# A causal attention with per-query maxima: scores in fp32r head pairs, double-bank exponentials and one loading queue

## The reference

```
q, k = rope(split_heads(x @ Wq.T + bq)), rope(split_heads(x @ Wk.T + bk))   # 16 heads of 16
v    = split_heads(x @ Wv.T + bv)
att  = softmax(causal_mask(q @ k.T / 4))
y    = (att @ v) @ Wo.T + bo
x    = layernorm(x + y)
h    = silu((x @ w1.T) * s1) * ((x @ w2.T) * s2)           # 1024 wide
h    = gelu((h @ h1.T) * hs1); h = gelu((h @ h2.T) * hs2)
out  = layernorm(x + (h @ w3.T) * s3)
```

## Time and profile before

| | |
|---|---|
| median of three runs | 3186.88 us (3184.31 to 3187.11) |
| profiled execution, first to last instruction | 3187.4 us (it has no other time of its own) |
| mean granted TensorE clock | 0.951 of full speed |
| projection | 0 to about 172 us |
| stacks loaded, TensorE idle | to 238 us |
| row scores alone | 238 to 329 us |
| groups of the attention | 329 to 1966 us |
| feed-forward stages | to 3187 us |

### The profile page before, as it was taken

How to read it: one execution, slowest core, us unless ns; L and a number is a source line. 1 busy time by engine, 2 the same in 40 slices (tenths; PEclk the granted TensorE clock), 3 DMA queues, 4 the chain that set the end, 5 groups by cost and what they waited for, 6 DMA issues and landing times. The chain is left out here.

```text
span 3187.4 us, 51027 instructions
## 1 busy us (share of the span) xinstructions
PE 2923.3 (92%) x15876; PEld 1538.9 (48%) x15876; DVE 2145.0 (67%) x3822; ACT 1310.6 (41%) x2546; POOL 145.8 (5%) x215
## 2 busy tenths in 40 slices
PE   8909999999999999999999997399999995799998
PEld 4402333333333333333333332277777774688887
DVE  7919888888888878888788885655555551434433
ACT  0000677777777766777767764011111110011010
POOL 0070000002000020000200000000000000000000
PEclk9955999999999999999999998699999998899999
DMA  5488000007100062000340001211111003121200
GB/s 158 151 112 99 9 8 5 5 5 81 32 5 5 6 68 45 5 5 6 47 63 8 5 6 64 92 53 53 53 53 53 33 34 127 59 74 39 79 14 20
DMA packets 80648, 146.59 MB, mean 46 GB/s; under 512 B 27452, under 2 KB 50876, under 8 KB 76840
## 3 DMA queue, kind: packets, MB, share of 16 engines
q0 software_dynamic: 11440, 45.43, 10.5%
q1 hardware_dynamic: 60344, 77.47, 7.2%
q10 hardware_dynamic: 8640, 20.85, 2.0%
HBM read 92.67 MB, written 51.04 MB: 45 GB/s over the span
## 5 line engine op out<-in xcount | busy, mean ns | idle before, releaser
L477 DVE TENSOR_REDUCE at_segmax<-at_row 128x1 f32<-128x512 f32 (+3 forms) x2464 | 1414.3, 636 | 315.5 <-PE at_row L393 181.3
L550 ACT ACTIVATE at_probs<-at_key 128x512 f32<-128x512 f32 (+3 forms) x2304 | 1141.9, 566 | 626.6 <-PE at_key L411 349.8
L393 PE MATMUL at_row<-at_k_stack,at_q_stack 96*128 96x512 bf16 (+3 forms) x2464 | 910.4, 378 | 98.5 <-DMA at_k_stack<-k_parts 75.2
L411 PE MATMUL at_key<-at_q_stack,at_k_stack 99*128 99x512 bf16 (+3 forms) x2304 | 831.4, 363 | 4.1 <-issue 1.6
L393 PEld LDWEIGHTS at_row<-at_k_stack,at_q_stack 96*128 96x128 bf16 x2464 | 237.2, 98 | 785.7 <-DVE at_segmax L477 590.9
L428 PE MATMUL at_o<-at_probs,at_values 128*32 128x512 f32 (+3 forms) x4608 | 572.7, 569 | 1.4 <-issue 0.7
L411 PEld LDWEIGHTS at_key<-at_q_stack,at_k_stack 99*128 99x128 bf16 x2304 | 225.8, 98 | 145.9 <-ACT at_probs L550 16.8
L1005 PE MATMUL na_h<-na_h_h,na_h2w_h 128*128 128x512 f32 x512 | 203.3, 397 | 46.2 <-DVE na_h_l L1058 46.2
L1043 ACT ACTIVATE na_h3f<-na_h,na_hs 128x512 f32<-128x512 f32 x64 | 44.0, 688 | 442.6 <-PE na_h L1005 442.6
L739 PE MATMUL wi_f<-wi_h_h,wi_h1w_h 128*128 128x512 f32 x512 | 207.4, 405 | 10.5 <-DVE wi_h_l L870 10.5
L1005 PE MATMUL na_h<-na_h_l,na_h2w_h 128*128 128x512 f32 x512 | 203.2, 397 | 0.0
(11 more groups left out here) (109 smaller groups left out, 2578.6 us busy)
## 6 DMA issues: line engine op xcount, KB each, us to landing
hidden<-wi_h SPq DMA_DIRECT2D x64, 256.0 KB, 2.0
na_h2f<-hidden SPq DMA_DIRECT2D x8, 2048.0 KB, 8.4
at_q_stack<-q_parts POOLq DMA_DIRECT2D x120, 128.0 KB, 25.5
at_k_stack<-k_parts POOLq DMA_DIRECT2D x30, 512.0 KB, 30.6
outputs<-at_outs POOLq DMA_DIRECT2D x32, 256.0 KB, 2.3
wi_o<-outputs SPq DMA_DIRECT2D x8, 1024.0 KB, 5.8
q_parts<-pr_parts SPq DMA_DIRECT2D x48, 128.0 KB, 1.9
k_parts<-pr_parts SPq DMA_DIRECT2D x48, 128.0 KB, 2.2
```

The source lines that it names most:

```text
L393: last = nc.tensor.matmul(bank[:, 0:w], qst[u][0:SROWS, c, h, i * P:(i + 1) * P], kst[u][0:SROWS, h, s * CH:s * CH + w], start=True, stop= ...
L411: last = nc.tensor.matmul(bank[:, q0:CH], kst[u][0:SROWS + PARTS, h, j * P:(j + 1) * P], qst[u][0:SROWS + PARTS, c, h, q0:CH], start=True, ...
L477: nc.vector.tensor_reduce(segmax[:, r, s:s + 1], row_ps[slot][:, 0:w], op=ALU.max, axis=AX.X).then_inc(rows_taken, 1)
L550: nc.scalar.activation(probs[:, g % RING_P, h, q0:CH], key_ps[(QUAD * g + h) % RING_S][:, q0:CH], ACT.Exp).then_inc(probs_ready, 1)
```

## The change

`project` splits q and k into two fp32r parts (high and low) instead of three bf16 ones, and stores them with 4 bytes an element. GpSimd also makes a tile of ones that is stored to DRAM.

`attend` is rewritten:

- `TERMS` are three (high by high, high by low, low by high): 48 rows for a head. Two heads lie over each other, at partitions 0 and 64, so a quad is two pairs. The stacks are fp32r. The maxima are two more rows (high, low) at 48 and 112.
- A key unit is a pair of heads: two matmuls into the two banks of one double bank, then one exponential over both (1024 columns). There are two double banks. Row units stay single, the two heads of a pair alternating, with three banks. Masks are bf16 as before.
- `values` follows two groups behind the keys instead of one, with four buffers of exponentials.
- The maxima are split on GpSimd, turned by VectorE (`transpose` of 32 x 32 blocks, six row units after the last one of the chunk), and stored by SyncE with four DMAs and loaded with two.
- All loads of stacks, ones and values move from GpSimd's queue to SyncE's. The first quad comes in pieces of 512 tokens, then quad 1 whole; only then follow the stores of maxima in SyncE's list.
- The quads run alternately up and down over the chunks. The order of row units and key pairs is worked out by a function `interleave` with fixed costs per instruction: at a chunk's first group all row units still missing for that chunk are issued, and further ones as long as a bank is free while the keys wait.
- There are no hardware loops in the attention: all is written out.

```diff
-PARTS = 3
-TERMS = [(0, 0), (0, 1), (1, 0), (1, 1), (0, 2), (2, 0)]
+PARTS = 2
+TERMS = [(0, 0), (0, 1), (1, 0)]
+RING_R = 3
+RING_K = 2
+PAIRS_G = QUAD // 2
+RING_P = 4
+VALUE_LAG = 2
...
+        parts = sb("parts", [P, 2, PARTS, CH], F32R)
...
-                            nc.vector.tensor_tensor(rest[:, :], full[:, :], parts[:, s, 0, :],
-                                                    ALU.subtract).then_inc(step, 1)
-                            dve.wait_ge(step, steps + 3)
-                            nc.vector.tensor_copy(parts[:, s, 1, :], rest[:, :]).then_inc(parts_ready, 1)
-                            dve.wait_ge(parts_ready, it * 4 * PAIRS + 2 * m + 1)
-                            nc.vector.tensor_tensor(parts[:, s, 2, :], rest[:, :], parts[:, s, 1, :],
+                            nc.vector.tensor_tensor(parts[:, s, 1, :], full[:, :], parts[:, s, 0, :].bitcast(F32),
                                                     ALU.subtract).then_inc(parts_ready, 1)
...
+def interleave(blocks, rows, groups):
+    last_row = {n: r for r, (n, *_) in enumerate(rows)}
+    before = []
+    pe = dve = act = 0.0
+    row_end, key_end, max_ready = [], [], {}
+    r = k = 0
+    while k < PAIRS_G * len(groups):
+        n, j = groups[k // PAIRS_G]
+        key_at = key_end[k - RING_K] if k >= RING_K else 0.0
+        row_at = row_end[r - RING_R] if r >= RING_R else 0.0
+        if r <= last_row[n] or (r < len(rows) and row_at <= max(pe, key_at, max_ready[n]) and row_at <= max(key_at, max_ready[n])):
+            m, i, p, s, _ = rows[r]
+            w = row_width(blocks[m][1], i, s)
+            pe = max(pe, row_at) + 0.3 * w + 15.0
+            dve = max(dve, pe + 200.0) + w * 1.04 + 60.0
+            row_end.append(dve)
+            if r == last_row[m]:
+                max_ready[m] = dve + 9000.0
+            r += 1
+            continue
+        before.append(r)
+        w = min(CH, CH - (j * P - blocks[n][1] * CH))
+        pe = max(pe, key_at, max_ready[n]) + 0.6 * w + 30.0
+        act = max(act, pe + 200.0) + 2 * w * 0.833 + 90.0
+        key_end.append(act)
+        if k % PAIRS_G == PAIRS_G - 1:
+            pe += 950.0
+        k += 1
+    return before
...
+        qst = [sb(f"q_stack{u}", [P, 2, T], F32R) for u in range(2)]
+        kst = [sb(f"k_stack{u}", [P, 2, T], F32R) for u in range(2)]
+        row_ps = [ctx.enter_context(nc.psum_tensor(f"at_row{i}", [P, CH], F32)) for i in range(RING_R)]
+        key_ps = [ctx.enter_context(nc.psum_tensor(f"at_key{i}", [P, 2, CH], F32)) for i in range(RING_K)]
...
+            def load_stacks(u, quad, t0, t1, loaded):
+                q_v = qp_d.rearrange("a (q p b d) t -> a q b d p t", q=NQUAD, p=2, b=2, d=HD)
+                k_v = kp_d.rearrange("a (q p b d) t -> a q b d p t", q=NQUAD, p=2, b=2, d=HD)
+                for b in range(2):
+                    for r, (qa, ka) in enumerate(TERMS):
+                        part = slice(64 * b + r * HD, 64 * b + (r + 1) * HD)
+                        sp.dma_start(qst[u][part, :, t0:t1].bitcast(F32), q_v[qa, quad, b, :, :, t0:t1]).then_inc(loaded, 16)
+                        sp.dma_start(kst[u][part, :, t0:t1].bitcast(F32), k_v[ka, quad, b, :, :, t0:t1]).then_inc(loaded, 16)
...
+            def store_max(n):
+                u, c = blocks[n][0] % 2, blocks[n][1]
+                sp.wait_ge(negrows_ready, n + 1)
+                for k in range(TPC):
+                    sp.dma_start(max_d[n].rearrange("b a p (i k x) -> (b a p i) k x", k=4, x=32)[:, k, :],
+                                 negrows[32 * k:32 * k + 32, n % 2, :]).then_inc(max_spilled, 16)
+                sp.wait_ge(max_spilled, 64 * (n + 1))
+                if n >= 4:
+                    sp.wait_ge(max_stored[n % 4], 32 * (n // 4))
+                for b in range(2):
+                    sp.dma_start(qst[u][64 * b + SROWS:64 * b + SROWS + 2, :, c * CH:(c + 1) * CH].bitcast(F32), max_d[n, b]
+                                 ).then_inc(max_stored[n % 4], 16)
...
+            load_stacks(0, 0, 0, CH, first_loaded[0])
+            load_ones(0)
+            load_values(0, 0)
+            for c in range(1, NCH):
+                load_stacks(0, 0, c * CH, (c + 1) * CH, first_loaded[c])
+            load_ones(1)
+            load_stacks(1, 1, 0, T, stacks_loaded[1])
+            load_values(1, 1)
+            done = 0
+            for g in range(NG):
+                for p in range(PAIRS_G):
+                    for r in range(done, before[PAIRS_G * g + p]):
+                        n = rows[r][0]
+                        if r == last_row[n]:
+                            store_max(n)
+                    done = before[PAIRS_G * g + p]
+                if g in out_after:
+                    store_out(out_after[g])
+                    quad, c = blocks[out_after[g]]
+                    if out_after[g] % NCH == NCH - 1 and quad + 2 < NQUAD:
+                        sp.wait_ge(probs_used, last_group[out_after[g]] + 1)
+                        load_stacks(quad % 2, quad + 2, 0, T, stacks_loaded[quad + 2])
+                        load_values(quad % 2, quad + 2)
...
+            def row_unit(r):
+                if r >= RING_R:
+                    pe.wait_ge(rows_taken, r - RING_R + 1)
+                part = slice(64 * b, 64 * b + SROWS)
+                last = nc.tensor.matmul(bank[:, 0:w], qst[u][part, p, q], kst[u][part, p, k], start=True, stop=(s < c))
+                if s == c:
+                    last = nc.tensor.matmul(bank[:, w - P:w], mask[:, :], ident[:, :], start=False, stop=True)
+                last.then_inc(rows_ready, 1)
...
+                for b in range(2):
+                    part = slice(64 * b, 64 * b + SROWS + 2)
+                    last = nc.tensor.matmul(bank[:, b, q0:CH], kst[u][part, p, j * P:(j + 1) * P],
+                                            qst[u][part, p, c * CH + q0:(c + 1) * CH], start=True, stop=(j < TPC * c))
+                if j >= TPC * c:
+                    for b in range(2):
+                        last = nc.tensor.matmul(bank[:, b, q0:q0 + P], ident[:, :], mask[:, :], start=False, stop=True)
+                last.then_inc(keys_ready, 1)
...
+                    if j == 0 and p == 0:
+                        pe.wait_ge(max_stored[n % 4], 32 * (n // 4 + 1))
...
+                for p in range(PAIRS_G):
+                    m = PAIRS_G * g + p
+                    act.wait_ge(keys_ready, m + 1)
+                    nc.scalar.activation(probs[:, g % RING_P, 2 * p:2 * p + 2, q0:CH], key_ps[m % RING_K][:, :, q0:CH],
+                                         ACT.Exp).then_inc(probs_ready, 1)
```

More of the change, by code:

```diff
@@ L262, in attend @@
-def attend(nc, io, qp_d, kp_d, v_d, max_d, o_d):
-    groups, units, LEAD, ahead, order = attend_plan()
-    NG = len(groups)
-    NU = len(units)
-    body_work, body_turn, body_copy, body_done = spread(order, NG - 4, NG)
-    pre_work, pre_turn, pre_copy, pre_done = spread([(0, x) for x in ahead], LEAD // 4, LEAD // 4 + 3)
-    RING_S = 3
-    RING_P = 3
-    MR = PARTS * QUAD * TPC
+    blocks = []
+    for quad in range(NQUAD):
+        blocks += [(quad, c) for c in (range(NCH) if quad % 2 == 0 else reversed(range(NCH)))]
@@ new lines, in attend_plan, with row_width @@
+    rows = [(n, i, p, s, b) for n, (_, c) in enumerate(blocks) for i in range(TPC) for p in range(2) for s in range(c + 1)
+            for b in range(2)]
+    groups = [(n, j) for n, (_, c) in enumerate(blocks) for j in range(TPC * (c + 1))]
+    return blocks, rows, groups
+def row_width(c, i, s):
+    return CH if s < c else (i + 1) * P
+def interleave(blocks, rows, groups):
[27 more added lines that the diff above has]
+    return before
@@ L272, in attend @@
+def attend(nc, io, qp_d, kp_d, ones_d, v_d, max_d, o_d):
+    blocks, rows, groups = attend_plan()
+    before = interleave(blocks, rows, groups)
+    NB = len(blocks)
+    NG = len(groups)
+    NR = len(rows)
+    last_row = {n: r for r, (n, *_) in enumerate(rows)}
+    last_group = {n: g for g, (n, _) in enumerate(groups)}
+    out_after = {min(g + VALUE_LAG, NG - 1): n for n, g in last_group.items()}
     with ExitStack() as ctx:
@@ L414, in key_unit, with values @@
                 if j >= TPC * c:
-                    last = nc.tensor.matmul(bank[:, q0:q0 + P], ident[:, :], mask[:, :], start=False, stop=True)
+                    for b in range(2):
+                        last = nc.tensor.matmul(bank[:, b, q0:q0 + P], ident[:, :], mask[:, :], start=False, stop=True)
                 last.then_inc(keys_ready, 1)
-            def values(u, g, quad, first):
-                c, j = groups[g]
+            def values(g):
+                n, j = groups[g]
+                quad, c = blocks[n]
+                u = quad % 2
@@ L421, in values @@
                 q0 = max(0, j * P - c * CH)
[L422 to L425 removed]
+                if j == 0 and n > 0:
+                    pe.wait_ge(out_taken, n)
+                if j == 0 and n % NCH == 0:
```

(24 more changed lines are left out.)

349 lines of the change are left out of this document (119 added, 230 removed).

## The result

| | before | after |
|---|---|---|
| median of the runs, us | 3186.99 (3184.31 to 3187.22) | 3491.36 (3459.62 to 3508.89) |
| span of the profiled execution, us | 3187.4 | 3500.0 |
| mean granted clock | 0.951 | 0.839 |
| attention's first DMA | 176 | 158.1 |
| first and last key score | 329.1, 1964.6 | 284.4, 2283.1 |

The ratio is 1.094 [1.089, 1.100]: 304 us slower, where 181 were forecast. That is inside the range of 3070 to 3690, and just outside the 3270 to 3480 of the likeliest case. The runs of the changed kernel spread over 1.4%, the longer the lower their mean clock (3460 us at 0.852, 3509 at 0.835); its profile, on which the readings rest, is 9 us above the median.

What follows compares the result with a forecast made beforehand. TensorE was taken to set the attention's pace, before and after. First key 303, bursts 338, steady groups 1380, clock 66, middle 57 and tail 2 end it at 2146 against 1965; 3187.4 + 181 = 3368 us, range 3070 to 3690.

Steps and rivals of the forecast that it cites:

- the likeliest case: The prediction's main case for the whole kernel, 3368 us: chance 0.5, own range 3270 to 3480 us.
- Projection: Before the attention: two VectorE steps per pair go, TensorE becomes late next; 13 us gained, attention's first DMA at 163.
- Until the first key score: Attention's start: maxima queue behind 14.9 MB at 111 GB/s, 134 us, then small DMAs, 6 us; first key at 303.
- Bursts and middle: Row scores in bursts at VectorE's pace, 338 us, and a standstill behind quad 3's load in mid-attention, 57 us.
- Steady groups: Attention outside bursts, TensorE-bound: values 639, keys 349, rows the rest; 1380 us, 2.5 for each of 555 groups.
- The prediction's aside: Masks in the attention: without the drain at a change of shape they would cost 46 us and not 237.
- Clock: After bursts in the attention: clock at half costs 3.3 us each, taken 20 times, 66 us.
- tail: End of the attention: one pair's exposed stores, 2 us.
- Rival 1: Attention: a change of shape costs no more than the old 0.09 and the clock holds; 3065 us, chance 0.2.
- the 2.16 to 2.9 that the prediction allowed: Sign for steady groups: the prediction is wrong if they take under 2.16 or over 2.9 us.
- Rival 2: Attention's score matmuls: the two row halves don't run at once; steady groups 1718 us, total 3706 us, chance 0.2.
- Rival 3: SyncE's queue loads at 250 GB/s: 74 us less at the start, 37 in the middle; 3257 us, chance 0.1.

Runs made afterwards that it cites:

- e5_probe: Changed kernel plus three matmul streams (one half's row scores, pairs on both halves, 128-row mask-sized) in TensorE's idle time before the first keys; 3484.86 us, one run.
- e6_same_half: Changed kernel with both heads of a key pair reading the lower half of the partitions (wrong operands for the second head); 4575.15 us, one run.
- e12_pieces_row_pairs: Kernel with loads in pieces, row scores now issued two heads together, each pair behind one wait for both its banks; 3499.24 us.
- e4_even_rows: Changed kernel with row scores dealt evenly over the groups, a chunk ahead and 18 more, instead of in bursts; 3532.15 us.

## Why the prediction was right, and where it was short

The direction held, and so did the costs that make it: two standstills for the maxima, bursts at VectorE's pace, and masks between one-half scores. Taking away the standstills gives back 142 us and taking away the masks 277, together more than the 304 that the change costs (no run had both). The time came out 123 us over. By its own steps:

- **Projection.** Forecast 13 us, measured 18 (176 to 158.1).
- **Until the first key score.** Forecast 303, measured 284.4: 14.9 MB came in some 122 us, at 148 and then 110 GB/s where 111 was taken throughout. The standstill was 85 us of TensorE, forecast 90. Loads in pieces show it caused by the order in the queue.
- **Bursts and middle.** Forecast 338 + 57, and the keys and values of these 20 groups, which the prediction counts with the steady ones (some 33 us): 428, measured 441. The middle's interval is 62 us (1273.1 to 1335.4).
- **Steady groups.** Forecast 1380, less those 33: 1347. Had all 555 run as they do at full clock, 428 x 2.36 + 127 x 2.74 would be 1358. A plain group's median is 2.14. The halves overlap, 4 ns apart, 0.23 a pair in e5_probe's stream. From the values to the next score it is 1.00 and not 1.18, so the weight load does hide there; but from the last pair to the values it is 0.33 to 0.43 (the medians of two kinds of group), 0.1 to 0.2 above a pair's own 0.23, where 0.09 was taken. The mask on one-half scores costs 0.30 more than on 96-row ones, where 0.29 was forecast for the change of shape. Small errors that cancel, which is luck in part. (The prediction's aside that the masks would cost 46 us without the change is some 54 by its own terms, 256 x 0.12 + 381 x 0.06; its sum doesn't use it.)
- **Clock, the term that was mis-sized.** Forecast 66 us, 3.3 behind each burst, from the 6 us of the earlier trace rows. Measured 1550 - 1358 = 192 in the groups between bursts. Behind a burst it stays at half for a median of 17 us (20 behind block 7's) and not 6. Before, what followed the row scores was 96-row matmuls; after, it is a mix, and of the 20 us behind block 7's burst 18 row scores on one half are some 7 us (0.43 for one of 512 columns). e5_probe and e6_same_half show that such work, however dense, leaves the clock at half. The prediction had read the clock as a matter of TensorE's idle time and had no term for how much of it works. That the one-half work is what makes 17 us of 6 is an inference: the same mix runs on at full clock once it is there (763 to 828 us), and e12_pieces_row_pairs, with all row scores in pairs, has a median of 11 us behind its bursts for 14 in the loads in pieces.

The account: -19 (first key), +9 (from the first key to the first values), +24 (bursts and groups at full clock: 441 + 1358 against 1775), +126 (clock), -2 (tail): with rounding 139, and 2285 against 2146 for the end of the attention. The stages behind it are 7 us shorter than before, and the median is 9 below the profile: 123.

Rival 1 (free changes of shape, clock holds) fails on both conditions, with 0.30 us a change and 192 us of clock. Without masks the change is still 27 us over the kernel before (3214, one run). The groups outside the bursts take 2.79 us each on the mean and 2.45 as they run at full clock, inside the 2.16 to 2.9 that the prediction allowed. Rival 2 (halves one after the other) is excluded by the 4 ns, and e6_same_half, where the key scores alone share one half, takes 4575, far over the 3706 given, for the clock again. Rival 3 is excluded by 110 GB/s.

**Open.** Why the clock rises in one stretch of a mix and not in another: in e4_even_rows TensorE passes 72 us at half clock from 386 with pairs and row scores in turn and 70.76 us busy, and groups of the same content run at full clock elsewhere. And no arrangement tried reaches the kernel before (best: 3348). A kernel in which row scores too use all 128 rows wasn't tried.

## What to carry to other kernels

A matmul that occupies one half of TensorE's rows saves time only next to its partner; a dense stream of them alone leaves the clock at half (0.50 over 33 us in e5_probe), so count the granted clock as a term of its own, from a stretch with the same kind of matmul. A mask over all rows between matmuls on half of them costs 0.30 us beyond its own work here; count the changes of shape before choosing the shape. Put small transfers that the compute waits for ahead of bulk loads in a shared queue: of all edits that keep the result only that one paid (142 us). Before dealing work evenly, check that the engine with the slower pace can be fed while the other is in a long step; four maxima a group made VectorE the bound at 2.94 us, three left it under 2.14.

## What the hardware showed that was not expected

- 48-row matmuls of one half, back to back: granted clock 0.50 for 33 us at 100% busy (e5_probe); pairs of both halves: full some 7 us after they begin.
- With both heads in one half the clock is at half for 2930 of 3064 us of attention (e6_same_half); TensorE is 99% busy in the stretch from 400 to 800 us.
- Two fp32r matmuls of 512 columns on two halves start 4 ns apart, and in a stream of pairs both together take 0.23 us; a 128-row mask between one-half matmuls costs 0.30 us more than between 96-row ones, some 0.2 out and 0.1 back.
